# Two layers of graph attention on one core: squares of a kernel matrix folded into the turned summands, and work reordered between four engines

## What is computed

```python
x = _layernorm(x + _L0_gnn_ref(x, adj, L0_gnn_bias), axis=-1)     # h
zn = z_l / jnp.maximum(jnp.linalg.norm(z_l, axis=-1, keepdims=True), EPS)
A_l = jnp.maximum(jnp.einsum('bnd,bmd->bnm', zn, zn), 0.0) * not_eye
d2 = jnp.maximum(sq + jnp.swapaxes(sq, -1, -2) - 2.0 * jnp.einsum('bnd,bmd->bnm', z_g, z_g), 0.0)
A_g = jnp.exp(-d2 / (2.0 * sigma * sigma)) * not_eye
K = w_l * K_l + (1.0 - w_l) * K_g          # row-normalised, causal A_l and A_g
out = jnp.einsum('bnm,bmd->bnd', K, v)
```

## Time and profile before

| what | us |
|---|---|
| median of 3 runs | 951.38 (951.23 to 953.14) |
| the profiled execution, own time | 956.53 |
| its span | 954.8 |
| PE busy | 921.0 (96%) |
| DVE busy | 752.5 (79%) |
| ACT busy | 535.4 (56%) |
| POOL busy | 312.8 (33%) |
| mean granted clock of PE | 0.989 |

### The profile page before, as it was taken

How to read it: one execution, slowest core, us unless ns; L and a number is a source line. 1 busy time by engine, 2 the same in 40 slices (tenths; PEclk the granted TensorE clock), 3 DMA queues, 4 the chain that set the end, 5 groups by cost and what they waited for, 6 DMA issues and landing times.

```text
span 954.8 us, 19036 instructions
## 1 busy us (share of the span) xinstructions
PE 921.0 (96%) x6858; PEld 542.5 (57%) x6858; DVE 752.5 (79%) x1716; ACT 535.4 (56%) x976; POOL 312.8 (33%) x435
## 2 busy tenths in 40 slices
PE   8999899899999999999999999999999999999993
PEld 7777787455555555556464646455555455555451
DVE  5887488768888888878787888888887878786766
ACT  6887556685555555555546464646373636463531
POOL 5888162244040404040505050505050504040410
PEclk9999899999999999999999999999999999999997
DMA  7554120001323232314141413232222323231211
GB/s 301 187 204 150 43 90 25 34 32 21 80 67 78 67 83 60 95 48 109 34 120 28 115 33 109 40 103 46 96 53 90 57 86 60 85 56 45 56 45 44
DMA packets 101848, 75.84 MB, mean 79 GB/s; under 512 B 80560, under 2 KB 80688, under 8 KB 99888
## 3 DMA queue, kind: packets, MB, share of 16 engines
q1 hardware_dynamic: 101808, 75.32, 27.4%
HBM read 38.86 MB, written 16.78 MB: 58 GB/s over the span
## 4 chain that ended last, share of the span: by engine, by line
issue 51%; PE 21%; POOL 14%; DVE 8%; ACT 5%; DMA 1%; POOLq 1%; DVEq 0%; ACTq 0%
POOL arena L438 6%; PE bank L265 2%; PE bank L267 2%; PE bank L266 2%; PE bank L538 2%; POOL arena L443 2%; POOL arena L477 2%; PE bank L545 1%; PE bank L544 1%; ACT arena L1188 1%; POOL rn_parts L460 1%; DVE stats L1692 1%; POOL part_rest L458 1%; PE bank L508 1%; PE pair L265 1%
## 5 line engine op out<-in xcount | busy, mean ns | idle before, releaser
L265 PE MATMUL bank<-arena 128*128 128x512 f16 (+2 forms) x1056 | 293.8, 302 | 7.3 <-DVE arena L1746 2.7
L267 PE MATMUL bank<-arena 128*128 128x512 f16 (+2 forms) x1056 | 293.5, 302 | 0.0
L266 PE MATMUL bank<-arena 128*128 128x512 f16 (+2 forms) x1056 | 293.5, 302 | 0.0
L265 PE MATMUL pair<-arena 128*128 128x512 f16 (+1 forms) x400 | 151.1, 378 | 0.0
L266 PE MATMUL pair<-arena 128*128 128x512 f16 (+1 forms) x400 | 150.8, 377 | 0.0
L267 PE MATMUL pair<-arena 128*128 128x512 f16 (+1 forms) x400 | 150.7, 377 | 0.0
L265 PEld LDWEIGHTS bank<-arena 128*128 128x128 f16 x1056 | 103.5, 98 | 69.4 <-DVE arena L1746 5.0
L267 PEld LDWEIGHTS bank<-arena 128*128 128x128 f16 x1056 | 103.7, 98 | 63.3 <-issue 0.3
L266 PEld LDWEIGHTS bank<-arena 128*128 128x128 f16 x1056 | 103.7, 98 | 54.7 <-issue 0.3
L460 POOL TENSOR_TENSOR sq_parts<-cf,zero 128x4 bf16<-128x4 f32 x16 | 3.3, 208 | 399.4 <-DVE cf L1795 399.4
L438 POOL TENSOR_TENSOR arena<-arena 128x512 f32<-128x512 f32 x64 | 81.0, 1267 | 60.2 <-ACT arena L1098 59.8
(11 more groups left out here) (344 smaller groups left out, 1943.0 us busy)
## 6 DMA issues: line engine op xcount, KB each, us to landing
arena<-in_x SPq DMA_DIRECT2D x32, 1024.0 KB, 5.5
out_dram<-arena SPq DMA_DIRECT2D x15, 1024.0 KB, 4.3
arena<-arena SPq DMA_TRANSPOSE x75, 3.2
arena<-in_x SPq DMA_DIRECT2D x2, 512.0 KB, 4.6
arena<-in_w_grav_t SPq DMA_DIRECT2D x1, 1024.0 KB, 7.3
arena<-in_w_lang_t SPq DMA_DIRECT2D x1, 1024.0 KB, 5.2
arena<-in_w_v SPq DMA_DIRECT2D x1, 1024.0 KB, 8.2
arena<-in_w_o_t SPq DMA_DIRECT2D x1, 1024.0 KB, 9.1
```

The lines of the kernel that those rows point to most:

```text
L265: pe.matmul(dst, ah, bh, start=start, stop=False)
L266: pe.matmul(dst, ah, bl, start=False, stop=False)
L267: return pe.matmul(dst, al, bh, start=False, stop=stop)
```

## The change

- **Second squares.** They no longer go through POOL, PE, ACT and PE. DVE reads the half product in bank 5 when `half_products(1)` is out, takes its diagonal (`diag_g`, `cf[1]`), and writes `dev` = bank 5 less that diagonal, row by row. ACT and DVE make the parts of `dev` instead of the bank's, so that `add_turned(1)` brings the transposed summand with its square subtracted. The factor of ACT's exponential is changed to fit (`HK`, `HALF_DOWN`). `sq_parts`, `sq_rows` and five matmuls a group go.
- **Inverse norms** still go over the products, but from the half product's diagonal (times 2), ahead of `add_turned(0)`, and PE asks for their parts behind mix(1).
- **PE**: mix(0) ahead of both `add_turned`; the four spreading matmuls inside mix(2).
- **ACT**: Ln and Exp of the norms ahead of `add_bias(0)`, the copy of the rows ahead of `add_bias(1)`, `first_roots(1)` ahead of `v_high(0)`, the copy of K ahead of `first_norm(2)`.
- **POOL**: the residual of item 0, then `inverse_parts`.
- **DVE**: the four `x_low` spread out, `first_stats` of items 2 and 3 later, `k_mix` ahead of `first_factors(1)` and `v_low(0)`.
- **Group 0**: the bias is added to x on ACT (`x_biased`) among the upper products, and y is made by DVE alone (`first_y`).
- **Start**: `ident_b` is made before `ident_neg`; the semaphores of adj's two parts are one.

The diff, cut to its core:

```diff
-    M_DOWN, HALF_DOWN = 2.0 ** -16, 2.0 ** -5
+    M_DOWN, HALF_DOWN = 2.0 ** -16, 2.0 ** -6
...
+            def inverse_parts(g):
+
+                wait(pool, s["rn_rows_ps"], g)
+                pool.wait_ge(s["r_ready"], g + 1)
...
             def body(g, slot, has_next):
-                pool.wait_ge(s["dg_ready"], g * 2 + 2)
-                part(g, cf[:, 1, :], sq_parts, s["sq_rows_ps"], (s["part_steps"], 0), s["sq_parted"])
                 if has_next:
                     residual(g + 1, 1 - slot, 0)
-                pool.wait_ge(s["r_ready"], g + 1)
-                pool.wait_ge(s["sq_parted"], g + 1)
-                part(g, nl[:, 5, :], rn_parts, s["rn_rows_ps"], (s["part_steps"], 4), s["rn_parted"])
+                inverse_parts(g)
                 if has_next:
                     residual(g + 1, 1 - slot, 1)
                     residual(g + 1, 1 - slot, 2)
-
                 pool.wait_ge(s["cf_ready"], g + 1)
                 wait(pool, s["kT_in"], g * 16)
                 pool.tensor_tensor(k_g, a_g, per_item(cf[:, 7, :]), ALU.mult).then_inc(s["kg_ready"], 1)
...
             def body(g, slot, has_next, has_second):
...
+                between(0)
                 pe.wait_ge(s["half_g_l_ready"], g + 1)
                 add_turned(1, s["gg_ps"])
-                between(0)
                 pe.wait_ge(s["half_l_l_ready"], g + 1)
                 add_turned(0, s["gl_ps"])
-                between(1, range(0, 1))
-
-                pe.wait_ge(s["sq_parted"], g + 1)
-                part_rows(0, sq_parts, s["sq_rows_ps"])
-                between(1, range(1, 3))
-                squares_along(g)
-                between(1, range(3, KB))
-                between(2)
-
-                pe.wait_ge(s["rn_parted"], g + 1)
-                part_rows(P, rn_parts, s["rn_rows_ps"])
-                between(3, range(0, 2))
+                between(1)
+                part_rows(g)
+                between(2, range(0, 2))
                 inverses_along(g)
-                between(3, range(2, KB))
+                between(2, range(2, KB))
+                between(3)
...
+            def x_biased(items):
+                act.activation(xg[0][:, items, :], xg[0][:, items, :], ACT.Identity,
+                               bias=bias_c[:]).then_inc(s["x_biased"], 1)
+
+            act.wait_ge(s["x_in0"], 16)
+            act.wait_ge(s["small_in"], 64)
+            x_biased(slice(0, HALF))
             for d in range(KB):
                 upper_out(1, d)
+            x_biased(slice(HALF, GB))
...
-                half_high(1, s["half_g_ps"], s["half_g_h_ready"])
-                half_high(0, s["half_l_ps"], s["half_l_h_ready"])
+                half_high(1, dev, s["dev_ready"], s["half_g_h_ready"])
+                half_high(0, bank[4][:].rearrange("p (b n) -> p b n", b=GB), s["half_l_ps"], s["half_l_h_ready"])
+                log_exp(g, nl, s["nl_in"], s["nl_log"], s["nl_exp"])
                 if has_next:
                     add_bias(g + 1, 0)
...
+                act.wait_ge(s["gg_ps"], g + 1)
                 act.wait_ge(s["hk_ready"], g + 1)
                 wait(act, s["graph_steps"], g * 4)
                 for b in range(GB):
                     ex = act.activation(e_g[:, b, :], bank[5][:, b * P:(b + 1) * P], ACT.Exp,
                                         scale=c1(KAPPA), bias=cf[:, 0, b:b + 1])
                 ex.then_inc(s["e_ready"], 1)
+                act.wait_ge(s["rn_rows_ps"], g + 1)
+                wait(act, s["rm_ps"], g)
+                act.activation(rn_rows[:], bank[6][0:GB * PARTS, 0:P], ACT.Copy).then_inc(s["rn_rows_ready"], 1)
                 if has_next:
                     add_bias(g + 1, 1)
                     add_bias(g + 1, 2)
-                act.wait_ge(s["rn_rows_ps"], g + 1)
-                wait(act, s["rm_ps"], g)
-                act.activation(rn_rows[:], bank[6][0:GB * PARTS, P:2 * P], ACT.Copy).then_inc(s["rn_rows_ready"], 1)
                 if has_next:
                     first_roots(g + 1, 0)
                     add_bias(g + 1, 3)
                     first_norm(g + 1, 1 - slot, 0)
                     first_norm(g + 1, 1 - slot, 1)
+                if has_next:
+                    first_roots(g + 1, 1)
                 v_high(0)
                 if has_next:
-                    first_roots(g + 1, 1)
-                    first_norm(g + 1, 1 - slot, 2)
                     act.wait_ge(s["k_ready"], g + 1)
                     act.activation(k_parts[:, 0:GB, :], k_mix, ACT.Copy, scale=K_UP).then_inc(s["kT_h_ready"], 1)
+                    first_norm(g + 1, 1 - slot, 2)
                     first_norm(g + 1, 1 - slot, 3)
                 v_high(1)
...
             first_roots(0, 0)
             first_norm(0, 0, 0)
             first_norm(0, 0, 1)
-            add_bias(0, 3)
+            first_roots(0, 1)
+            hT_high(0)
+            hT_high(1)
+            first_norm(0, 0, 2)
+            first_norm(0, 0, 3)
+            hT_high(2)
+            hT_high(3)
...
-            first_roots(0, 1)
-            upper_out(0, 0)
-            first_norm(0, 0, 2)
-            first_norm(0, 0, 3)
-            for b in range(GB):
-                hT_high(b)
-            for d in range(1, KB):
+            for d in range(KB):
                 upper_out(0, d)
...
                 if has_second and has_previous:
-                    x_low(g + 2, slot, range(0, HALF))
+                    x_low(g + 2, slot, range(0, 1))
...
-                if has_second:
-                    x_low(g + 2, slot, range(HALF, GB) if has_previous else range(GB))
-
-                half_low(1, s["half_g_h_ready"], s["half_g_l_ready"])
-                dve.wait_ge(s["gg_ps"], g + 1)
+
+
+                dve.wait_ge(s["half_g_ps"], g + 1)
                 dve.tensor_tensor(diag_g, gg, for_items(ident[:]), ALU.mult).then_inc(s["dg_ready"], 1)
-                half_low(0, s["half_l_h_ready"], s["half_l_l_ready"])
                 dve.wait_ge(s["dg_ready"], g * 2 + 1)
                 dve.tensor_reduce(cf[:, 1, :], diag_g, AX.X, ALU.add).then_inc(s["dg_ready"], 1)
                 dve.wait_ge(s["dg_ready"], g * 2 + 2)
+                dve.tensor_tensor(dev, gg, per_item(cf[:, 1, :]), ALU.subtract).then_inc(s["dev_ready"], 1)
                 dve.tensor_scalar(cf[:, 0, :], cf[:, 1, :], c1(HK), None, ALU.mult).then_inc(s["hk_ready"], 1)
-
-                dve.wait_ge(s["gl_ps"], g + 1)
+                if has_second:
+                    x_low(g + 2, slot, range(1 if has_previous else 0, 2))
+                dve.wait_ge(s["half_g_h_ready"], g + 1)
+                half_low(1, dev, s["half_g_l_ready"])
+
+                dve.wait_ge(s["half_l_h_ready"], g + 1)
                 dve.tensor_tensor(diag_l, gl, for_items(ident[:]), ALU.mult).then_inc(s["nl_steps"], 1)
+                half_low(0, gl, s["half_l_l_ready"])
                 dve.wait_ge(s["nl_steps"], g * 2 + 1)
                 dve.tensor_reduce(nl[:, 5, :], diag_l, AX.X, ALU.add).then_inc(s["nl_steps"], 1)
                 dve.wait_ge(s["nl_steps"], g * 2 + 2)
-                dve.tensor_scalar(nl[:, 0, :], nl[:, 5, :], 1e-18, None, ALU.max).then_inc(s["nl_in"], 1)
-
-                dve.scalar_tensor_tensor(t_l, gl, 0.0, for_items(mask[:]), ALU.max, ALU.mult).then_inc(gs, 1)
+                dve.tensor_scalar(nl[:, 0, :], nl[:, 5, :], 2.0, 1e-18, ALU.mult, ALU.max).then_inc(s["nl_in"], 1)
+                if has_second:
+                    x_low(g + 2, slot, range(HALF, HALF + 1))
                 newton(g, nl, s["nl_exp"], s["nl_steps2"], nl[:, 3, :], 3).then_inc(s["nl_steps2"], 1)
                 dve.wait_ge(s["nl_steps2"], g * 3 + 3)
                 dve.tensor_scalar(nl[:, 5, :], nl[:, 3, :], c1(CAP_C), None, ALU.min).then_inc(s["r_ready"], 1)
...
+                dve.wait_ge(s["gl_ps"], g + 1)
+                dve.scalar_tensor_tensor(t_l, gl, 0.0, for_items(mask[:]), ALU.max, ALU.mult).then_inc(gs, 1)
...
                 if has_next:
                     first_stats(g + 1, 1)
                     first_moments(g + 1, 0)
-                    first_stats(g + 1, 2)
+                if has_second:
+                    x_low(g + 2, slot, range(HALF + 1, GB))
+                if has_next:
                     first_factors(g + 1, 0)
...
                 if has_next:
-                    first_stats(g + 1, 3)
-                    first_moments(g + 1, 1)
+                    first_stats(g + 1, 2)
...
                 if has_next:
-                    first_factors(g + 1, 1)
-                v_low(0)
-
+                    first_stats(g + 1, 3)
+                    first_moments(g + 1, 1)
                 dve.wait_ge(s["cl_ready"], g + 1)
                 dve.wait_ge(s["kg_ready"], g + 1)
                 for b in range(GB):
                     last = dve.scalar_tensor_tensor(k_mix[:, b, :], a_l[:, b, :], cf[:, 3, b:b + 1], k_g[:, b, :],
                                                     ALU.mult, ALU.add)
```

(15 more changed lines are left out.)

143 lines of the change are left out of this document (60 added, 83 removed).

## The result

The changed kernel takes 968.6 us (median of 4 runs, 965.3 to 970.7), the one before 951.3 on the same chip: ratio 1.017, interval 1.014 to 1.020. It is **slower**, by 17 us, where 947.4 and "faster" were forecast. The time lies just inside the range (931 to 970), close to what rival 2 gave.

What follows compares the result with a forecast made beforehand. TensorE, busy 96%, was taken as the bound. Terms -11.2 - 2.7 + 16.5 - 3.4 - 2.5 - 0.7 = -4.0 gave 952.5 us profiled, 947.4 us median; range 931 to 970, from rival 1 (no stall) to rival 2.

Steps and rivals of the forecast that it cites:

- rival 2: POOL and DVE block each other's steps, the turn of K lands late, PE waits 1.3 us: 970 us; chance 28%.
- The matmuls saved: On PE, five products fewer per group for the squares' rows and their spreading: 0.70 us in each of 16 groups, -11.2 us.
- the wait for `z_low`: PE's wait ahead of half_products(0) goes, as one x_low moves from in front of z_low(0, 0): -2.7 us.
- `dev` costs nothing: On the second squares' longer chain, DVE's dev, 0.69 us a group, counts nothing, with 1.9 us to spare.
- The stall at part_rows: PE, behind mix(1), waits 0.8 to 1.4 us for the inverse norms' parts in 15 groups: +16.5 us, between +12 and +21.
- The start of group 0: y by DVE alone, bias in ACT's pauses; PE's 2.18 us idle and half-clock stretch go: -3.4 us, bounds 0 and -4.2.
- The last group: PE's 2.62 us wait goes, the second wait grows by some tenths: -2.5 us, bounds 0 and -5.
- The wait for h ahead of it: PE's wait of 1.8 us for h ahead of the last group shrinks as PE comes later: -0.7 us.
- Behind PE's wait stand mix(2) and all that follows: In the inverse norms' part: mix(2) and all later work stand behind PE's wait for the parts; no separate size given.
- The other half of that sentence: Behind ACT's wait for the rows stands add_bias(1), which then runs at 509.1 as it does now.
- a difference that the forecast carried over unchanged: The profiled execution before, 956.53 us, against the runs' median of 951.38: 5 us, carried over unchanged to the forecast.

Runs made afterwards that it cites:

- c1: b2 with VectorE's last x_low(g + 2) moved between k_mix and kT_l: 937.3 us, 0.9847 of the kernel before.
- a1: The changed kernel with GpSimd's inverse_parts(g) put ahead of residual(g + 1, 0): 976.8 us, 1.023 of the kernel before.
- a2: The changed kernel with part_rows behind half of mix(2), the spread behind its second half, ScalarE's rows copy behind add_bias(1): 966.5 us, 1.014 of the kernel before.
- b1: The kernel before with only the start of group 0 changed (x_biased, first_y, new order, one semaphore for adj's parts): 949.2 us against 953.0, 0.9967.
- a3: The changed kernel with GpSimd's subtraction low_h cut to 4 columns of 512, part of the computation left out: 949.4 us, 0.9955 of the kernel before.
- a4: The changed kernel with VectorE's four xw_low(g + 2) behind the four second_residual(g) instead of ahead: 956.3 us, 1.0022 of the kernel before.
- d2: c1 with part_rows, the spread and the copy of the rows back in the changed kernel's places: 972.4 us, 1.0197 of the kernel before.
- b2: The changed kernel with most of the body in the order of before, squares turned and group 0's start kept: 957.4 us, 1.0051 of the kernel before.

## Why the prediction was wrong

- **The matmuls saved and the wait for `z_low`** (-11.2, -2.7): right. In c1, where nothing else binds, the period fell by 0.85 us, where 0.70 + 0.17 were forecast.
- **`dev` costs nothing**: right (c1), as long as the chain isn't stretched.
- **The stall at part_rows** (+16.5): there, and of the right size: 15 waits, 16.2 us. Its cause is right too, residual(0) ahead of the parts, with two details missed: L1770 is held beside residual(0), so the inverse norms come at 507.26, not 505.8, and the last part is held beside a_g, the worst place. But a1 and a2 show that in this kernel it was not what alone set the time: with it taken away, the kernel won 2 us or lost 8.
- **The start of group 0** (-3.4): -3.8 (b1). **The last group** (-2.5): 2.2 us of waits less. Right. The wait for h ahead of it (-0.7) was wrong in sign: it is 2.2 us now and was 1.8.
- **The step that failed** is in the part on the inverse norms: "Behind PE's wait stand mix(2) and all that follows". These were let go as a delay that everything shares, and the sum has no term for the chain of statistics, roots, norms, v_high and v_low to second_residual. With VectorE's held steps and its new order (moments(1) behind the coefficients) that chain comes back to TensorE 1.15 us late in each of 14 groups: 16 us that the sum of -4.0 lacks. a3 and a4 each take this wait away, for 19 and 12 us. The other half of that sentence, on ScalarE's wait and add_bias(1), did no harm: add_bias(1) ran at 509.60 instead of 509.1, statistic 1 stood where it did, and a2, which puts add_bias(1) ahead of the copy again, wins only 2 us in all.
- **The size.** -4.0 + 16 = +12, against +17.3 in the medians (13 to 19 by the interval). The spans' 11.2 come near only because the profiled execution of before was slow: it lies 5.2 us above its median, a difference that the forecast carried over unchanged. Without the lost clock, at most 3.4 us, the traces give 11.2 + 3.4 = 14.6. Some 3 to 5 us are thus in no term.
- **d2** prices the early place where no other wait is left: +35 us instead of the +16.5.
- **Rival 2** had the mechanism, and the forecast erred in making it an alternative of all or nothing, with the stretched steps at zero in the sum. They did not miss each other: the rows put residual(2) and k_g beside first_factors(0), and there they were. That held steps cost time is shown by a3. Its time, 970, is near the 968.6, but this is luck in part, for its place was wrong: it had the turn of K land 1.3 us late. first_factors(0) ended at 516.19, not 517, L325 (the turn of K) went out at 524.51, not 525.4, and TensorE hardly waited for a DMA, 0.5 us between 240 and 900. What was late next was VectorE's queue: moments(1), now behind the coefficients, held roots, norms and v_high(1) back, and four xw_low stood ahead of second_residual. a4 shows that queue, 12 us.
- The Trainium skill's rule (SBUF — State Buffer, "SBUF: two separate sides"), by which VectorE with two SBUF inputs and GpSimd exclude each other for a whole instruction, agrees with the stretched rows of two such inputs (L1669, L1672, L1807, L1813, and x_low and a_g in a2 and a1) and spoke for rival 2. The stretched `tensor_scalar` rows (L1770, L1661) read one tensor, and that case of the rule does not cover them.

What stays open: the 3 to 5 us above, and the share of the single moves in the 11 us between the changed kernel and b2. x_low's place is the same in both; the early place of part_rows and the order of roots and statistics were not parted there.

## What to carry to other kernels

A wait on the bound engine doesn't shift all that follows alike. Other engines' chains start behind it, and if they are stretched or reordered on the way they come back late and are waited for again (d2: 13.6 us and 16.8 us). Follow each chain to where it comes back to the bound engine before calling the rest covered. And when steps are reordered on a nearly full VectorE, lay GpSimd's large steps beside it on one time axis: here a step of 0.16 us with two SBUF inputs that started beside one lasted until that ended, up to 1.2 us, so where a filler step goes can be worth more than the work that the change saves. A change that loses may only stand in the wrong order: the squares turned, mostly in before's order and with one step moved, won 1.5% (c1, with the new start of group 0).

## What the runs showed of the hardware

The rows show which of VectorE's steps are held beside GpSimd's, and for how long. Held until GpSimd's step ends: small steps with two inputs in SBUF (0.15 to 0.22 us by themselves, 0.95 to 1.22 held) and the `tensor_scalar` steps L1770 (0.23 by itself in the last group, 1.32 held) and L1661 of b2 (1.08 held). Large steps with two SBUF inputs wait and then run: x_low, 0.75 us, took 1.76, and a_g, 0.67, took 1.61. Not held, in the midst of a residual of GpSimd (516.10 to 517.38): a step whose second large input is a bank (a_l, L1800, 0.68) and the one-input reduction (L1803, 0.69). It works the other way as well: in a2 k_g lasted 1.49 us instead of 1.04 behind x_low, and in the changed kernel GpSimd's last part 0.57 instead of 0.20 beside a_g.
